# The output product of attention: four fp32 products a group, or one in fp32r halves with w_out standing

## What is computed

```python
tokens = einsum('bnpd,edp->bne', patches, Wr) + b          # 64 x 93 x 128
xn = layernorm(layernorm(h)) * gamma + beta
q, k, v = (three-tap convolution over time of (w1 @ xn))   # 512 rows each
attn = softmax(q k^T * scale + alibi, causal)
out = (attn @ v).transpose(0, 2, 1, 3).reshape(b, n, 512)
h = h + out @ wout.T                                       # the product that is changed
logits = layernorm(h) @ gate_weight.T                      # top 2 of 16 experts
h_mean = mean over an expert's tokens of silu(x @ w1.T);  y_mean = h_mean @ w2.T
h = h + sum over the token's two experts of weight * y_mean
```

## Time and profile before

| | |
|---|---|
| median of 3 runs | 800.21 us (799.69 to 801.07) |
| profiled execution | 802.93 us |
| its span | 801.3 us |
| TensorE busy | 747.2 us, 93% |
| VectorE busy | 620.6 us, 77% |
| ScalarE busy | 471.6 us, 59% |
| GpSimd busy | 375.4 us, 47% |
| granted TensorE clock | 0.977 |

### The profile page before, as it was taken

One profiled execution on the slowest core, in us unless ns is written; L12 is line 12 of the kernel. 1 busy time (PEld: TensorE's weight loads), 2 busy tenths in 40 slices (PEclk: granted clock), 3 DMA queues, 4 the chain that ended last, 5 costly groups with the idle time before them and its releaser, 6 DMA issues.

```text
span 801.3 us, 20507 instructions
## 1 busy us (share of the span) xinstructions
PE 747.2 (93%) x6674; PEld 690.3 (86%) x6674; DVE 620.6 (77%) x1645; ACT 471.6 (59%) x998; POOL 375.4 (47%) x390
## 2 busy tenths in 40 slices
PE   4678999999999999999999999998998879899987
PEld 4568999999999999999999999997786778799982
DVE  2255878888888888888888888898987569788855
ACT  3444666656565656665565656555553377699940
POOL 3643233766555565656564555654443453122200
PEclk9988999999999999999999999999999989999989
DMA  6421132332211112211221111111124112122205
GB/s 187 138 75 40 40 110 94 101 102 67 55 51 50 48 49 55 65 47 49 51 67 52 48 50 50 50 27 56 44 67 167 30 39 78 41 64 66 60 11 153
DMA packets 44269, 53.97 MB, mean 67 GB/s; under 512 B 13651, under 2 KB 31251, under 8 KB 43696
## 3 DMA queue, kind: packets, MB, share of 16 engines
q1 hardware_dynamic: 30048, 38.84, 17.0%
q0 software_dynamic: 12544, 12.87, 5.8%
q10 hardware_dynamic: 1616, 1.48, 0.6%
HBM read 42.69 MB, written 10.26 MB: 66 GB/s over the span
## 4 chain that ended last, share of the span: by engine, by line
PE 76%; DVE 10%; ACT 4%; issue 3%; DMA 2%; POOL 2%; DVEq 1%; ACTq 1%; SPq 0%
PE ps L452 10%; PE psO L590 9%; PE ps L453 8%; PE ps L454 8%; PE psO L672 6%; PE psS L612 6%; PE psS L538 4%; PE ps L524 3%; PE psO L718 3%; PE psV L557 3%; PE ps L718 3%; PE psV L635 2%; PE psS L607 2%; DVE qkv L972 2%; DVE qkv L975 2%
## 5 line engine op out<-in xcount | busy, mean ns | idle before, releaser
L1331 POOL DMA_INDIRECT expert_rows<-hn,slot x128 | 168.0, 1313 | 67.9 <-DVE slot L1172 35.5
L1264 POOL TENSOR_TENSOR x_lo<-x_raw,x_hi 128x752 fp32r<-128x752 f32 x64 | 114.9, 1797 | 141.7 <-ACT x_hi L777 141.7
L972 DVE SCALAR_TENSOR_TENSOR qkv<-ps,taps,qkv 128x368 f32<-128x368 f32 x192 | 113.9, 593 | 73.6 <-ACT qkv L785 69.0
L785 ACT ACTIVATE qkv<-ps,taps 128x372 f32<-128x372 f32 x192 | 108.7, 567 | 88.1 <-PE ps L454 85.5
L975 DVE SCALAR_TENSOR_TENSOR qkv<-ps,taps,qkv 128x364 f32<-128x364 f32 x192 | 114.6, 597 | 6.8
L452 PE MATMUL ps<-x_hi,wtok_hi 128*128 128x376 f32 x256 | 94.4, 369 | 14.0 <-DVE wtok_lo L960 9.1
L590 PEld LDWEIGHTS psO<-vrow,probT 93*93 93x93 f32 x1024 | 93.9, 163 | 4.8 <-ACT probT L827 3.2
L590 PE MATMUL psO<-vrow,probT 93*93 93x65 f32 x1024 | 94.3, 246 | 2.1 <-DVE resid L1107 0.8
L453 PE MATMUL ps<-x_lo,wtok_hi 128*128 128x376 f32 x256 | 88.0, 344 | 0.0
L454 PE MATMUL ps<-x_hi,wtok_lo 128*128 128x376 f32 x256 | 87.6, 342 | 0.0
L452 PE MATMUL ps<-xnT_hi,wqkv_hi 128*128 128x372 f32 x192 | 77.5, 404 | 8.2 <-DVE qkv L975 5.0
(11 more groups left out here) (197 smaller groups left out, 1582.5 us busy)
## 6 DMA issues: line engine op xcount, KB each, us to landing
x_raw<-in_x SPq DMA_DIRECT2D x64, 376.0 KB
w1s<-in_w POOLq DMA_DIRECT2D x8, 512.0 KB
w<-in_w SPq DMA_DIRECT2D x4, 1024.0 KB
out<-resid SPq DMA_DIRECT2D x16, 160.0 KB, 2.4
xsE<-expert_rows SPq DMA_DIRECT2D x36, 64.0 KB, 1.8
xs<-expert_rows SPq DMA_DIRECT2D x36, 64.0 KB, 1.8
xs<-expert_rows POOLq DMA_DIRECT2D x36, 64.0 KB, 2.1
expert_rows<-hn,slot POOLq DMA_INDIRECT x128
```

Of the source, the lines that this page charges most:

```text
L785: nc.scalar.activation(qkv[u][:, k, :, :], psP[(k + 1) % 2][:, 0:GT].rearrange("p (b n) -> p b n", n=NT), ACT.Copy, scale=taps[:, k, 2:3]) ...
L972: nc.vector.scalar_tensor_tensor(dst[:, :, 1:NT], src[:, :, 0:NT - 1], taps[:, k, 1:2], dst[:, :, 1:NT], ALU.mult, ALU.add).then_inc(tap1_ ...
L1264: nc.gpsimd.tensor_tensor(x_lo[u][:, 0:PIECE], x_raw[u][:, :], x_hi[u][:, 0:PIECE].bitcast(F32), ALU.subtract)\
L1331: nc.gpsimd.indirect_dma_start(rows, bass.IndirectOffsetOnAxis(slot[1 - u][:, c:c + 1], 0), hn[1 - u][:, c % GB, :], None)\
```

## The change

Each batch's transposed attention is now split in fp32r halves: ScalarE writes `attnT_hi` (`attn_high`), VectorE the rest `attnT_lo` (`attn_low`), each with room for the four batches of a group. Once a group, at s = 1 of the gate step, TensorE makes one product over 372 columns with `w_out`, split in halves too, as standing operand (`project_out`, 4 x 3 fp32r products into `psO`). The result has features on partitions; ScalarE copies it to `yT` (the buffer of `xnT`), TensorE transposes it back per batch (`turn_out`, into one of the banks of `proj`, which blocks 4 and 7 now wait for), and VectorE adds 93 x 512 at once. Around it work is moved: `turn_attn` (transposes of `attn`) to the end of quarters 1 to 3; value and `hn` transposes behind the probability product; the second norm's addition and statistics behind convolution 3s; `x_lo` ahead of the second norm's small terms on GpSimd; `tap2`, `normalise` and `tokT` on ScalarE reordered; `up_quad` of quad 0 and its `silu_quad` from s = 0 to s = 1 of t = 19; the memset of `mean` from behind the early quads to t = 19; the fetches of early tiles share a semaphore per quad. `w_out` is read into a spare part of `qkv` and split in t = 2.

```diff
-        attnT = sb("attnT", [128, QB, NT])
+        attnT_hi, attnT_lo = (sb(f"attnT_{part}", [128, QB, GB, NT], F32R) for part in ("hi", "lo"))
+        wout_hi, wout_lo = (sb(f"wout_{part}", [128, QB, D], F32R) for part in ("hi", "lo"))
...
+        yT = xnT
+        def psRes(t):
+            return psS[:NT, 0, :] if isinstance(t, int) and t == NG + 3 else psP[1][:NT, :]
+        def psHn(t):
+            return psS[:, 1, 0:GT] if isinstance(t, int) and t == NG + 3 else psP[0][:, 0:GT]
...
                 if k == 1 and f.norm:
                     wait(pe, res_evac, t)
+                if k == 4 and f.gate:
+                    wait(pe, res_add, t - 3)
+                if k == 7 and f.gate:
+                    wait(pe, hnT_evac, t - 3)
...
+            def turn_attn(f, s, n):
+                if f.attn:
+                    pe.wait_ge(v_evac, n + 1)
+                pe.wait_ge(norm_done, n)
+                for j in range(QB):
+                    mm = nc.tensor.transpose(psV[:, j * NT:(j + 1) * NT], attn[:, j * 128:(j + 1) * 128],
+                                             ident[:NT, :NT])
+                mm.then_inc(a_tr, 1)
+            def project_out(t):
+                wait(pe, a_lo_done, (t - 3) * GB)
+                if isinstance(t, int) and t == 4:
+                    pe.wait_ge(wout_lo_done, 1)
+                for j in range(QB):
+                    a_hi, a_lo = (a[:, j, :, :].rearrange("p b n -> p (b n)") for a in (attnT_hi, attnT_lo))
+                    mm = split_product(psYT, wout_hi[:, j, :], wout_lo[:, j, :], a_hi, a_lo,
+                                       start=(j == 0), stop=(j == QB - 1))
+                mm.then_inc(out_mm, 1)
+            def turn_out(t, f):
+                wait(pe, yT_evac, t - 3)
+                wait(pe, conv_done, (t - 2) * NBLK + 3 if f.proj else NG * NBLK)
+                for b in range(GB):
+                    mm = nc.tensor.transpose(psRes(t)[:, b * D:(b + 1) * D], yT[:, b * NT:(b + 1) * NT], ident[:, :])
+                mm.then_inc(y_tr, 1)
...
-                    if prev:
-                        pe.wait_ge(a_evac, n)
-                        if f.gate and s == 3:
-                            wait(pe, base_done, t - 3)
-                        for j in range(QB):
-                            mm = nc.tensor.matmul(psWout, attnT[:, j, :], wout[:, j, :],
-                                                  start=(j == 0), stop=(j == QB - 1))
-                        mm.then_inc(out_mm, 1)
-                    if q is not None and s == 0:
-                        up_quad(q, 0, QUAD)
+                    if prev and s > 0:
+                        turn_attn(f, s, n)
+                    if s == 1 and quad(t, 0) is not None:
+                        up_quad(quad(t, 0), 0, QUAD)
...
+            def attn_high(s, n):
+                ac.wait_ge(a_tr, n)
+                nc.scalar.activation(attnT_hi[:, :, (s - 1) % GB, :], psV[:, 0:GT].rearrange("p (j n) -> p j n", n=NT),
+                                     ACT.Copy).then_inc(a_hi_done, 1)
...
+            def attn_low(s, n):
+                dve.wait_ge(a_hi_done, n)
+                nc.vector.tensor_tensor(attnT_lo[:, :, (s - 1) % GB, :], psV[:, 0:GT].rearrange("p (j n) -> p j n", n=NT),
+                                        attnT_hi[:, :, (s - 1) % GB, :].bitcast(F32), ALU.subtract).then_inc(a_lo_done, 1)
...
                     if f.proj:
                         conv(t, u, 3 * s)
+                    if f.gate and s == 1:
+                        wait(dve, y_tr, t - 3)
+                        res = resid[:, bass.ds((t - 4) * (GB * D), GB * D)]
+                        nc.vector.tensor_tensor(res, psRes(t), res, ALU.add).then_inc(res_add, 1)
+                        wait_apart(dve, res_add, t - 3)
+                        stats(t - 4, stat2, mv2, ln2_stat, ln2_mv)
...
+                    if isinstance(t, int) and t == NG + 3 and s == 0:
+                        dve.wait_ge(v_tr, B)
+                        dve.wait_ge(s_mm, B)
+                        nc.vector.memset(mean, 0.0).then_inc(mean_zero, 1)
...
-                    if prev:
-                        dve.wait_ge(out_mm, n)
-                        res = resid[:, bass.ds((n - 1) * D, D)]
-                        nc.vector.tensor_tensor(res, psWout, res, ALU.add).then_inc(res_add, 1)
...
-            nc.vector.memset(mean[:, :, :], 0.0).then_inc(mean_zero, 1)
```

More of the change, by code:

```diff
@@ L77, in build @@
         taps = sb("taps", [D, NBLK, 3])
-        wout = sb("wout", [128, QB, D])
         wgate = sb("wgate", [D, E])
@@ L160, in build @@
         part = sb("part", [128, NTILE, FB])
-        act_e = act + [late[1][:, k * F:(k + 1) * F] for k in range(3)] + [late[1][:, 2336:2336 + F]]
+        act_e = act + [late[1][:, k * F:(k + 1) * F] for k in range(4)]
         NA = len(act_e)
@@ L573, in step @@
                         tok_taps(t, s, 0, 1)
+                    if f.gate and s == 1:
+                        turn_out(t, f)
                     if q is not None and s == 0:
@@ L599, in step @@
                         mm.then_inc(xnT_tr, 1)
+                    if f.attn:
+                        if s == 0:
+                            pe.wait_ge(conv_done, (t - 2) * NBLK)
+                        wait(pe, a_lo_done, n - 1)
+                        for j in range(QB):
+                            mm = nc.tensor.transpose(psV[:NT, j * 128:(j + 1) * 128],
+                                                     qkv[1 - u][:, 2 * QB + j, s, :], ident[:, :])
+                        mm.then_inc(v_tr, 1)
+                    if f.gate and s == 2:
+                        wait(pe, hn_ready, t - 3)
+                        wait(pe, conv_done, (t - 2) * NBLK + 6 if f.proj else NG * NBLK)
+                        for b in range(GB):
+                            mm = nc.tensor.transpose(psHn(t)[:, b * NT:(b + 1) * NT], hn[u][:, b, :],
+                                                     ident[:NT, :NT])
+                        mm.then_inc(hnT_tr, 1)
+                    if q is not None and s == 2:
+                        turn_quad(q)
                     if f.attn:
@@ L620, in step @@
                         tok_taps(t, s, 1, 2)
-                    if f.attn and prev:
-                        pe.wait_ge(v_evac, n + 1)
                     if f.scat and s == 0:
                         wait(pe, rw_done, t - 4)
-                        wait(pe, a_evac, n - 1 if prev else B)
+                        wait(pe, a_lo_done, n - 1 if prev else B)
+                        if f.attn:
+                            pe.wait_ge(v_evac, n + 1)
                         mm = nc.tensor.transpose(psRT, rw[:, :, :].rearrange("p b e -> p (b e)"),
@@ L630, in step @@
                             mm.then_inc(rwT_tr, 1)
-                    if prev:
+                    if prev and s == 0:
+                        turn_attn(f, s, n)
+                    if f.gate and s >= 2 and prev:
                         pe.wait_ge(norm_done, n)
-                        for j in range(QB):
-                            mm = nc.tensor.transpose(psV[:, j * NT:(j + 1) * NT], attn[:, j * 128:(j + 1) * 128],
-                                                     ident[:NT, :NT])
-                        mm.then_inc(a_tr, 1)
                     if f.gate and s == 2:
@@ L1057, in step @@
                         place(t - 5, 1 - u)
-                    if f.gate and s == 1:
-                        wait(dve, res_add, (t - 3) * GB)
-                        stats(t - 4, stat2, mv2, ln2_stat, ln2_mv)
-                        if not f.attn:
-                            sum_quad(0)
                     if f.gate and s == 3:
@@ L1297, in step @@
                         nc.gpsimd.tensor_tensor(shift[:, :], nmean[:, :], rstd[:, :], ALU.mult).then_inc(ln_shift, 1)
+                    if f.tok and f.more(t, s):
+                        low(t * GB + (s + 1), (s + 1) % 2)
                     if f.gate and s == 1:
```

137 lines of the change are left out of this document (69 added, 68 removed).

## The result

The changed kernel takes 829.06 us (median of 4 runs, 825.87 to 836.37) against 800.64 for the kernel before; the ratio is 1.036 (95% interval 1.033 to 1.039). The forecast was 810 (787 to 817): the direction and the place of the loss in the loop came out as written, the size did not. The profiled execution took 825.87 us, 823.8 of them its span, 22.5 more than the span before. The slowest run, at 836.37, had a mean granted clock of 0.945 where the profiled one had 0.969, so part of the loss differs from run to run.

A forecast was written before the change was run, and what follows sets the result against it. It took TensorE to bound the kernel, VectorE close behind. Head -3.5, loop +5.0, 512 to 634 us +7.1, t = 19 +3.2 and memset -1.7 sum to +10.1: 813.0 profiled, median 810.3, predicted 810, range 787 to 817.

The forecast's parts named there:

- t = 17 and 18: Last attention steps: VectorE's added work and waits behind project_out and turn_out cost +1.5 and +1.9 us.
- ring of VectorE: Loop: VectorE's chain from project_out to tok_tr sets the step, 37.0 against 36.56 us, +5.0 over 11 steps.
- the 30.0: Loop: VectorE ends convolution 11 at 30.0 us after the quarter's start, where tok_tr on TensorE waits for it.
- the 6.95: Loop: from tok_tr to the end of s = 0 takes 6.95 us, closing the step at 37.0.
- signs named: Loop profile if right: steps 36.8 to 37.3 us, gaps before block 6 and tokT, VectorE idle 2 us, busy 87 to 89%.
- TensorE's relief, -1.15 a step: Loop: TensorE's own work alone falls from 36.56 to 35.4 us a step.
- rival 1: Whole kernel: TensorE stays the only bound, loop step 35.4 us, -12.0 in all, 788 us; chance 0.28.
- t = 15 and 16: First two stretches after the loop, VectorE mostly full: its added work costs +1.7 and +2.0 us.
- Rival 4: Stalls also lower the granted clock: three more slow stretches of 2 us, +6 on the 810 us case, 816 us; chance 0.08.
- t = 19: Serial step ending attention: subtraction, product, yT and transposes replace the old product, +1.8 to +3.9, taken as +3.2 us.
- The memset, -1.7: Late tiles: memset of mean moves into idle VectorE time, so the first late tile starts earlier, -1.7 us or 0.
- Head, -3.5: Before the first project_out near 110 us: four output products leave while TensorE has no gap, -3.5 us.

The follow-up runs named there:

- e2: Changed kernel without the subtraction making attnT_lo, the 12 products reading attnT_hi instead (time only, result wrong); the loop was 2.89 us shorter.
- e1: Changed kernel with block 3 of the projections before the output product, and ScalarE's tap before its copy yT; 824.07 us.
- e15: Kernel before with four more VectorE copies a step into an unread tile; seven of 11 loop steps took 36.82 to 37.24 us, three 39.8 to 41.2.
- e10: Changed kernel with block 3 before the output product, first token tap before the tokT transposes, and wden on ScalarE; ratio 1.026 to the kernel before.
- e13: Changed kernel with only filler products added on TensorE in the last two steps of attention; ratio 1.026 to the kernel before.
- e4: Kernel before with only the memset of mean moved from the late tiles to t = 19, s = 0; ratio 0.996.
- e9: Changed kernel with one small operation, wden, moved from VectorE to ScalarE; loop 411.80 us, profiled time 836.52 us.
- e3: Changed kernel with 32 filler products of 128x384 on TensorE in t = 18; t = 18 took 23.36 us, t = 16 40.26.
- e8: Changed kernel with some 110 filler products on TensorE from t = 16 until attention ends; t = 16, 17 and 18 took 43.78, 34.09 and 23.30 us.
- e11: e10 with filler products on TensorE in the last two steps of attention only; 808.6 us, ratio 1.011.
- e14: Changed kernel with block 3 first, first token tap before the tokT transposes, filler in the last two attention steps, wden still on VectorE; loop 402.93 us.
- e5: Changed kernel with the second norm's statistics on VectorE and normalise on ScalarE moved behind block 5's work; 961 to 966 us together with two variants.

## Why the prediction was right and wrong

Two terms of the sum carry the miss. The clock in t = 17 and 18 was left out of the sum and cost at least 6.6 us; the loop was put at +5.0 and cost +9.45.

- **The loop, ring of VectorE: right in place, short in size (+9.45 for +5.0), and wrong as one ring.** Convolution 3 at 4.10 us after the quarter's start (4.1 forecast), convolution 4 at 10.10 (10.1), block 6 at 11.37, the `tokT` transposes at 30.54 (30.0), from there to the ring's end 7.12 (6.95). So the step is 37.66 rolled and 36.9 unrolled, 37.0 forecast. Mis-sized were the 30.0 (VectorE's waits for ScalarE's taps were 0.42 and 0.36 and not 0.5 together, and 0.14 passes between the last convolution and the transposes) and the 6.95 (the value transposes in front of bf16 work 0.46, not 0.36). Of the signs named, the gaps before block 6 and `tokT` released by the convolution came, and 2.06 us idle before convolution 3. The step came out above the 36.8 to 37.3 (411.82 / 11 = 37.44), VectorE at 356.01 / 411.82 = 86%, under the 87 to 89%.
- **One ring or several.** I wrote of one, with two subtractions in it at 0.9 us. Taking all four away gave 0.26 to 0.35 us a step (e2). e1 and e2 showed separate links that each hold TensorE for 0.3 to 0.6 us, so that taking one away does not give its own length. And the load needs no new order to cost something: e15's cost 0.4 a step.
- **TensorE's relief, -1.15 a step, was 0.77**: 35.8 us without its waits, not 35.4, and 35.9 with the order mended (e10). By the pieces alone, 3.48 out and 2.59 in, it was 0.9. It was not cashed in any order tried, so those orders don't show rival 1 (788 us).
- **t = 15 and 16: right**, +1.85 and +2.25 for +1.7 and +2.0.
- **t = 17 and 18: the step that failed.** +11.30 for +3.4. The sum priced them at the full clock. At full clock (e13) they are 57.40 - 52.67 = +4.7 with the filler in; the other 6.6 us are clock. Rival 4 named the mechanism and asked for three slow stretches of 2 us, and its price of 6 is near the 6.6; but it had a chance of 0.08 and stood outside the sum. What should have warned is how near these stretches of before already were: TensorE idle 13% in t = 17 and, in the window of t = 18, 21.12 - 17.53 = 3.6 us or 17%, at clocks of 1.00 and 0.99; and the change adds waits there.
- **t = 19**, +4.54 for +3.2. The products came at the slow pace that I had named as the other end, 0.31 us start to start:
```profile
665.64 0.68 PE L463 MATMUL psO<-attnT_hi,wout_hi 128*128 128x372 f32 x1 [1.29 <-DVE attnT_lo L1105]
666.11 0.51 PE L464 MATMUL psO<-attnT_lo,wout_hi 128*128 128x372 f32 x1
666.42 0.51 PE L465 MATMUL psO<-attnT_hi,wout_lo 128*128 128x372 f32 x1
```
  That is 3.9 us where the earlier trace rows had 1.90. In e13, whose filler reaches into s = 0 of t = 19, the pace fell too, from the third of the 12 on.
- **The memset, -1.7: by e4 -3.2** to the sixth tile (7.51 us from the first transposes against 10.73), half of it the shorter wait (1.57) and the rest the faster first tiles, which were priced at nothing. Another 2.0 us that the late tiles gained was not tested.
- **Head, -3.5:** 35.09 to 32.62 us from the first `shifted` transposes on, -2.5, and 32.63 to 32.67 in e9 and e13, the same program there. The 0.84 lost before them (75.48 against 74.64) is no more than executions differ in: e13 has 74.65 there and e9 76.18.
- **`attnT_lo`** was 0.535 us long and 0.45 to the next, as forecast from the earlier trace rows:
```profile
L1105 DVE TENSOR_TENSOR attnT_lo<-psV,attnT_hi 128x372 fp32r<-128x372 f32 x64 | 34.2, 535 | 2.8 <-ACT attnT_hi L840 2.8
```
- **`hn`**, against the earlier trace rows, was normalised at 342.04, 9.6 us after the quarter's start (9.4 forecast).

What stays open: why the clock falls in t = 16 in one execution and not in the next with the same program up to there (1.00, 0.95 and 0.83 in the profiles of the changed kernel, e13 and e3), and so how much of the difference between a profile and its median (829.06 to the profiled 825.87) is this.

## What to carry over

When the bound engine is relieved and its neighbour loaded, cost the step as a queue with places, not as sums: find each place where the neighbour's result is awaited and how long that result's own chain is, since closing one wait only uncovers the next. Where the bound engine already has gaps, a further wait can be paid twice, once as time and once as clock, as in t = 17 and 18 here; look at which stretches before the change have gaps at a clock that is still near 1.00 (here t = 17 and 18, at 1.00 and 0.99). Measure the engine's waits by distances, start to start, since its busy time hides them. And try the small part of a change by itself: here the moved memset was worth 0.4%, and the rest cost ten times that.

## What the runs showed of the hardware that I had not expected

- **Filling waits with useless products kept the clock.** It was 1.00 in t = 17 and 18 in e8, e11, e13 and e14, against 0.91 and 0.78; by the medians of e13 the kernel gained 8 us, by its profile 5.6. TensorE's clock fell behind stops of a different kind too, of 4.48 us (e8) and 6.14 (e5).
- **A small edit came with 8 us elsewhere.** e9 moved one operation of 93x4 elements, its loop is the same to 0.02 us, and its four runs took 833 to 839 us against 826 to 836, with clocks of 0.91, 0.75 and 0.71 in t = 16 to 18. Why the clock fell lower there was not tested.
- **VectorE stood still while GpSimd worked.** Changed kernel, VectorE and then GpSimd:
```profile
363.19 0.52 DVE L1224 TENSOR_SCALAR wden<-egap 93x4 f32<-93x4 f32 x1
363.75 0.17 DVE L1226 RECIPROCAL wts<-wden 93x4 f32<-93x4 f32 x1
```
```profile
362.46 1.28 POOL L1399 DMA_INDIRECT expert_rows<-hn,slot  x1 [0.30 <-issue]
```
  An operation that takes 0.15 us elsewhere ends 0.03 us before the end of GpSimd's instruction, 363.74. The Trainium skill ("SBUF — State Buffer", Who interferes with whom) says that a `tensor_scalar` in a mode that uses both ports holds a pair shared with GpSimd, and that whichever comes second waits for the whole of the other's instruction. These rows agree with it, others do not. Behind an unrolled step the same operation began 0.52 us into GpSimd's instruction and ran in 0.15 us inside it:
```profile
513.02 0.15 DVE L1224 TENSOR_SCALAR wden<-egap 93x4 f32<-93x4 f32 x1
```
```profile
512.50 1.28 POOL L1399 DMA_INDIRECT expert_rows<-hn,slot  x1 [0.30 <-issue]
```
  In e15 six of its kind began 0.3 us into such an instruction and took 0.15 to 0.16; those of the changed kernel that stood still began 0.7 us in. So in these runs GpSimd's instruction did not hold VectorE for its whole length. What made VectorE stand still was not tested, since e9 removed the operation and not the overlap.
- **A longer loop body came with stalls and more code loading.** In e15 VectorE idled 2.8 to 2.9 us once in each of three of the loop's four turns, with no releaser, and the page counts more packets on the second queue for instructions than that of the kernel before (26):
```profile
q14 instruction: 43, 0.34, 0.1%
```
  All other kernels here have 26. One such packet falls into each of the three idles, and from 240 to 460 us the queue had 16 where the kernel before had 1. Four instructions a step were added on VectorE. That the one causes the other was not tested.
